# Log attention on one Trainium2 core: the weighted values of a step stand ahead of its second row of scores on TensorE

## The chip, the cores and the metric

One core of a Trainium2 chip runs the whole program in one launch. The metric is the device time of that launch in microseconds. Three runs of the kernel before were timed; one further execution was taken with the hardware profiler.

## What is computed

The reference is four layers on x of shape (8, 512, 128), float32, each on a layernorm and added to x: linear attention, an expert layer, log attention, and the same expert layer again. The change lies in log attention:

```python
L = jnp.einsum('bhqd,bhkd->bhqk', q, k) * scale
mask = jnp.tril(jnp.ones((t, t), dtype=L.dtype))[None, None]
L_y = jnp.einsum('bhqd,bhkd->bhqk', q, k_y) * scale
agg = jnp.sum(jnp.exp(jnp.clip(L_y, -15.0, 15.0)) * mask, axis=-1, keepdims=True) + EPS
r = jnp.log(jnp.abs(L) + EPS) - jnp.log(agg + EPS)
w = jax.nn.softplus(r) * mask
A = w / (jnp.sum(w, axis=-1, keepdims=True) + EPS)
out = jnp.einsum('bhqk,bhkd->bhqd', A, v)
```

with 16 heads of 8, and t = 512.

## The kernel before

Each engine has its own instruction list, written out by hand and tied together by semaphores. Log attention runs in steps: ten steps (`DUS`, i = 0 to 9) make a batch, and eight batches make 80 steps (`STEPS_A`). A step handles one or two blocks of keys by queries (`PIECES`) for all sixteen heads. There are two sides. Side A (step n) makes q.k_y scores: ScalarE takes their exp (`exponential`, L1717), VectorE clips it (`clip_exps`, L1835), POOL masks it (L1949), and two steps later TensorE sums it over the keys (`sum_exps`, L1620). Side B runs sixteen steps later (m = n - DUS - LAG) on q divided by those sums: VectorE takes the absolute value of the scores out of psum (`abs_scores`, L1843), ScalarE takes log(1 + .) (`logarithm`, L1723), POOL masks, and TensorE multiplies with the values and with ones (`weight_values`, L1636), two steps later still. The rings `ring_a` and `ring_b` hold three steps each.

Scores of a step come in two rows (`scores`, L1588, u = 0 and 1), for two heads of four each. A row of one side fills a pair of psum banks. As soon as side B runs (n of 16 and over), side A has only the pair 0 and side B only the pair 1 (`score_banks`), so each row waits in `wait_scores` until ScalarE's exp and VectorE's abs have read the row before. The text calls the rows S0 and S1.

At the end of most steps stands something for a neighbouring batch, all of it in bank 7, and each user waits for the reader of the one before (`wait_shared_bank`): at i = 0 `project` of q2 (L1653), at i = 1 `project_out` (L1676, behind VectorE's `scale_q`, L1857), at i = 2 `turn` (L1645, behind `add_output`, L1897), at i = 3, 4, 5 `project` of q, ky and k (L1653), at i = 6 `project_v` (L1658), at i = 8 `sum_prefix` (L1667). ScalarE and VectorE split the q, ky and k into two parts (`split_high` L1733, `split_low` L1850), at i = 4, 5, 6; VectorE's `split_low` stands behind its second abs of the step. At i = 8 VectorE's `empty` stands ahead of its first abs, at i = 9 `divide` and `correct` close the step, at i = 0 `add_routed` (L1360). The split parts go through DRAM: SP stores them (L1983) and loads them into `stacks` (L1988) in a fixed order, each behind a wait.

From n = 80 on (k = n - 80) side A is over. Each step then carries a piece of the second expert layer: ScalarE normalises (L872) and copies turned rows (L878, L881), VectorE takes their low part (L1114), TensorE turns rows in `lead_turn` (L697) and makes router logits in `lead_tensor` (L708), VectorE works out the routing from k = 8 to 10 (`rows_of`, L1275), and from k = 11 POOL sends the rows to their experts (L1002), each send with a short memset behind it (L467), 24 sends for a first chunk of rows and 24 for a second. On POOL `send` stands behind the masks of its step.

Of the kernel before, what the change touches and what calls it, by code (L numbers as in the profile page):

```python
# [86 lines left out]
def build(nc, x_in, ins, out):  # L87

    ctx = ExitStack()
    with ctx:  # L90
# [422 lines left out]
        class NothingFollows:  # L513
            takes_rest = False

            def tensor_step(self, pe, n):
                pass
# [938 lines left out]
        STEPS_A = B * DUS  # L1456
# [50 lines left out]
        class LogAttention:  # L1507
# [172 lines left out]
            def tensor_step(self, pe, n):  # L1680
                (a, i), m = divmod(n, DUS), n - DUS - LAG
                in_a, in_b = 0 <= n < STEPS_A, 0 <= m < STEPS_A
                self.scores(pe, n, m, 0)
                if 0 <= n - 2 < STEPS_A:
                    self.sum_exps(pe, n - 2)
                self.scores(pe, n, m, 1)
                if 0 <= n - STEPS_A:
                    self.following.lead_turn(pe, n - STEPS_A)
                if 0 <= m - 2 < STEPS_A:
                    self.weight_values(pe, m - 2)  # L1690
                if i == 0 and 0 <= a - 1 < B:
                    self.project(pe, "q2", a - 1)
                if i == 1 and 0 <= a - 3 < B:
                    self.project_out(pe, a - 3)
                if i == 2 and a + 1 < B:
                    self.turn(pe, a + 1)
                if i in (3, 4, 5) and a + 1 < B:
                    self.project(pe, ("q", "ky", "k")[i - 3], a + 1)
                if i == 6 and 0 <= a < B:
                    self.project_v(pe, a)  # L1700
                if i == 8 and 0 <= a - 1 < B:
                    self.sum_prefix(pe, a - 1)
                if 0 <= n - STEPS_A:
                    self.following.lead_tensor(pe, n - STEPS_A)
# [455 lines left out]
```

## Time and profile before

| | us |
|---|---|
| median of 3 runs | 1372.37 |
| lowest, highest | 1367.05, 1372.8 |
| profiled execution, its own time | 1369.74 |
| its span, first to last instruction | 1368.0 |
| TensorE matmul busy | 938.6 (69%) |
| VectorE busy | 675.0 (49%) |
| ScalarE busy | 595.1 (44%) |
| POOL busy | 538.3 (39%) |
| granted TensorE clock, mean | 0.82 |

Engines: PE is TensorE, PEld its weight loads, DVE VectorE, ACT ScalarE, POOL GpSimd, SPq the SyncE queue that issues DMAs. A row of a timeline has the start, the length, the engine, the line of the kernel, the operation and its operands, how many instructions were merged (x), and in brackets the idle time before it with what ended that time. Merged rows that follow one another overlap by some hundredths of a microsecond, so a stretch is taken from start to start. The granted clock is a share of full speed: 1.00 is 2.4 GHz, 0.50 is 1.2 GHz, and a figure between is a mean over a stretch with both.

### The profile page before, as it was taken

What the parts mean: (1) busy time and instruction counts of PE and PEld (TensorE: products, weight loads), DVE (VectorE), ACT (ScalarE), POOL (GpSimd) and SP (SyncE); (2) the same over time, 40 slices, a digit from 0 to 9 for tenths busy, and PEclk for the clock granted to TensorE, in tenths of its full rate; (3) what the DMA queues carried; (4) which work ended last, traced back from release to release, by engine and by line L of the source; (5) the groups of instructions that cost most, each with busy time, mean ns of one, the idle gap of its engine ahead of it and who ended that gap; (6) DMA issues with size and microseconds to landing.
All of it is one profiled execution on the core that took longest, in us unless ns stands there. A gap on an engine that the chain in (4) does not pass through costs nothing.

```text
span 1368.0 us, 19627 instructions
## 1 busy us (share of the span) xinstructions
PE 938.6 (69%) x6851; PEld 558.7 (41%) x6851; DVE 675.0 (49%) x1408; ACT 595.1 (44%) x853; POOL 538.3 (39%) x711
## 2 busy tenths in 40 slices
PE   4678538775947457787878787787676727359970
PEld 3556427553725123233333333333343515336650
DVE  4778413510213144787777877777558413202332
ACT  1222113232514356677776867786533214125430
POOL 1110670182181143464533333333216770421865
PEclk9877558896978576799999999999657868679985
DMA  9300020022321444353534343330200210032332
GB/s 288 93 1 1 29 63 1 23 64 77 93 57 58 141 149 154 129 163 126 172 121 147 106 155 121 138 113 27 70 8 24 66 35 9 17 89 85 101 83 77
DMA packets 101837, 118.88 MB, mean 87 GB/s; under 512 B 9328, under 2 KB 64112, under 8 KB 101616
## 3 DMA queue, kind: packets, MB, share of 16 engines
q1 hardware_dynamic: 74800, 91.54, 20.3%
q0 software_dynamic: 8192, 16.79, 4.1%
q10 hardware_dynamic: 18752, 9.31, 2.3%
q8 instruction: 59, 0.97, 0.3%
q14 instruction: 34, 0.28, 0.1%
HBM read 59.60 MB, written 58.00 MB: 86 GB/s over the span
## 4 chain that ended last, share of the span: by engine, by line
PE 34%; POOL 18%; DVE 15%; DMA 12%; issue 10%; SPq 6%; ACT 3%; another core or an unknown queue 0%; POOLq 0%; DVEq 0%; ACTq 0%
POOL x_sorted L1002 8%; DVE ring_b L1843 6%; PE psum L777 6%; POOL pause_room L467 5%; DMA stacks<-stack_qr 5%; PE psum L1636 4%; PE psum L1588 4%; POOL r_rows L1010 4%; SPq L1988 3%; SPq L1983 3%; PE psum L800 3%; PE psum L740 2%; PE psum L751 2%; DMA stack_q<-parts 2%; DMA stacks<-stack_ky 2%
## 5 line engine op out<-in xcount | busy, mean ns | idle before, releaser
L1843 DVE TENSOR_SCALAR ring_b<-psum 128x1024 int32<-128x1024 int32 x160 | 195.7, 1223 | 116.7 <-PE psum L1588 116.7
L1717 ACT ACTIVATE ring_a<-psum 128x1024 f32<-128x1024 f32 x160 | 163.2, 1024 | 151.0 <-PE psum L1588 149.2
L1588 PE MATMUL psum<-stacks 32*128 32x128 f32 (+3 forms) x1024 | 107.6, 401 | 138.1 <-DVE ring_b L1843 92.2
L1002 POOL DMA_INDIRECT x_sorted<-r_rows,rows_of x128 | 124.2, 970 | 171.2 <-DVE rows_of L1275 136.1
L1723 ACT ACTIVATE ring_b<-ring_b 128x1024 f32<-128x1024 f32 x160 | 168.5, 1054 | 48.1 <-DVE ring_b L1843 48.1
L1949 POOL TENSOR_SCALAR_AFFINE_SELECT ring_b<-ring_b 128x512 f32<-128x512 f32 (+1 forms) x112 | 82.1, 746 | 271.8 <-ACT ring_b L1723 271.4
L1010 POOL DMA_INDIRECT r_rows<-y_sorted,rows_of x128 | 128.7, 1005 | 141.6 <-DMA y_sorted<-y_out 110.5
L1588 PEld LDWEIGHTS psum<-stacks 32*128 32x128 f32 x1024 | 63.0, 202 | 235.9 <-issue 88.1
L1341 DVE TENSOR_TENSOR ring_b<-psum,ring_b 128x512 f32<-128x512 f32 x72 | 49.1, 683 | 211.7 <-ACT ring_b L904 192.4
L777 PE MATMUL psum<-w_expert,ring_a 128*128 x284 | 140.9, 619 | 5.2 <-issue 3.5
L1835 DVE TENSOR_SCALAR ring_a<-ring_a 128x1024 f32<-128x1024 f32 x160 | 121.2, 761 | 41.5 <-ACT ring_a L1717 41.3
L1949 POOL TENSOR_SCALAR_AFFINE_SELECT ring_a<-ring_a 128x512 f32<-128x512 f32 (+1 forms) x112 | 84.1, 764 | 75.6 <-DVE ring_a L1835 75.6
L1636 PE MATMUL psum<-ring_b,values 128*32 128x256 f32 (+3 forms) x1024 | 111.9, 514 | 0.0
L1636 PE MATMUL psum<-ring_b,ones_s 128*32 128x256 f32 (+3 forms) x1024 | 109.4, 504 | 0.0
L1620 PE MATMUL psum<-ring_a,ones_s 128*32 128x256 f32 (+3 forms) x1024 | 96.4, 487 | 3.2 <-POOL ring_a L1949 2.5
L740 PE MATMUL psum<-stacks,w_shared 128*128 128x512 f32 x168 | 51.9, 458 | 54.3 <-DVE ring_b L1332 30.9
L904 ACT ACTIVATE ring_b<-psum 128x512 f32<-128x512 f32 x72 | 42.5, 591 | 106.6 <-PE psum L777 104.5
L800 PE MATMUL psum<-w_expert,ring_b 128*128 x568 | 79.7, 285 | 6.3 <-issue 2.9
L467 POOL MEMSET pause_room<- 128x384 f32 x184 | 79.6, 432 | 0.2
L800 PEld LDWEIGHTS psum<-w_expert,ring_b 128*128 128x128 f32 x568 | 73.2, 201 | 7.3 <-issue 7.3
L777 PEld LDWEIGHTS psum<-w_expert,ring_a 128*128 128x128 f32 x284 | 50.6, 199 | 44.1 <-issue 44.0
L790 PEld LDWEIGHTS psum<-identity,ring_b 128*128 128x128 f32 x284 | 37.1, 148 | 65.7 <-issue 36.1
(205 smaller groups left out, 1350.5 us busy)
## 6 DMA issues: line engine op xcount, KB each, us to landing
ring_a<-x_sorted SPq DMA_DIRECT2D x34, 256.0 KB
y_sorted<-y_out ACTq DMA_DIRECT2D x34, 256.0 KB
stack_q<-parts SPq DMA_DIRECT2D x32, 256.0 KB
stack_ky<-parts SPq DMA_DIRECT2D x32, 256.0 KB
stacks<-stack_q SPq DMA_DIRECT2D x32, 256.0 KB
stacks<-stack_ky SPq DMA_DIRECT2D x32, 256.0 KB
stack_k<-parts SPq DMA_DIRECT2D x32, 256.0 KB
stacks<-stack_k SPq DMA_DIRECT2D x32, 256.0 KB
```

What stands on the lines that cost most here:

```text
L467: nc.gpsimd.memset(pause_room[:], 0.0).then_inc(paused, 1)
L777: mm = nc.tensor.matmul(bank(2 * (k % 2) + m), x_turned[:, n % 2, (i % 4) * 128:(i % 4 + 1) * 128], w["w_expert"][:, bass.ds(columns[m], 2 ...
L800: mm = nc.tensor.matmul(tiles(bank(4))[:, i % 4, :], hidden_turned[:, j % 2, at:at + 128], w["w_expert"][:, bass.ds(self.columns[j][m] + ( ...
L1002: nc.gpsimd.indirect_dma_start(out=x_sorted, out_offset=bass.IndirectOffsetOnAxis(ap=rows_of[:, n, at + t:at + t + 1], axis=0), in_=x_rows ...
L1010: nc.gpsimd.indirect_dma_start(out=fetched[:, b % 4, n, t, :], out_offset=None, in_=y_sorted[0:pages_of(self.last_of(self.chunk_ending(b)) ...
L1588: mm = nc.tensor.matmul(bank(2 * pair + j % 2)[:, column:column + width], keys[rows, s, kb * 128:(kb + 1) * 128], queries[rows, s, q0:q0 + ...
L1636: mm = nc.tensor.matmul(psum[32 * j:32 * j + 32, into, q0:q0 + width], weight, ring[:, m % RING, j, column:column + width], start=i == 0, ...
L1717: nc.scalar.activation(exps[:, n % RING, 2 * u:2 * u + 2, :], psum[:, first:first + 2, :], ACT.Exp, scale=SCALE).then_inc(self.exp, 1)
L1723: nc.scalar.activation(part, part, ACT.Ln, bias=1.0).then_inc(self.ln, 1)
L1835: nc.vector.tensor_scalar(part, part, CLIP_LO, CLIP_HI, ALU.max, ALU.min).then_inc(self.clip, 1)
L1843: nc.vector.tensor_scalar(ring[:, m % RING, HEADS_B[u][0]:HEADS_B[u][1] + 1, :].bitcast(I32), psum[:, first:first + 2, :].bitcast(I32), 0x ...
L1949: ins = nc.gpsimd.affine_select(out=part, in_=part, pattern=[[0, part.ap[1][1]], [1, 128]], compare_op=ALU.is_ge, fill=0.0, base=0, channe ...
```

## The change

`tensor_step` issues `weight_values` of step m - 2 right behind `sum_exps`, ahead of the second row of scores, where it stood behind that row and behind `lead_turn`. Nothing else is changed; the lists of the other engines are the same.

```diff
                 self.scores(pe, n, m, 0)
                 if 0 <= n - 2 < STEPS_A:
                     self.sum_exps(pe, n - 2)
+                if 0 <= m - 2 < STEPS_A:
+                    self.weight_values(pe, m - 2)
                 self.scores(pe, n, m, 1)
                 if 0 <= n - STEPS_A:
                     self.following.lead_turn(pe, n - STEPS_A)
-                if 0 <= m - 2 < STEPS_A:
-                    self.weight_values(pe, m - 2)
                 if i == 0 and 0 <= a - 1 < B:
                     self.project(pe, "q2", a - 1)
```

On TensorE, step n = 44 (i = 4) from the end of its first row of scores to the projection of ky; L1588 are scores, L1620 the sums, L1636 the weighted values. Before:

```order
L1588 MATMUL psum<-stacks 128x128 x2
L1620 MATMUL psum<-ring_a,ones_s 32x512 x4
L1588 MATMUL psum<-stacks 128x256 x2
L1588 MATMUL psum<-stacks 128x384 x2
L1588 MATMUL psum<-stacks 128x256 x2
L1588 MATMUL psum<-stacks 128x128 x2
L1636 MATMUL psum<-ring_b,values 32x384 x4
L1636 MATMUL psum<-ring_b,ones_s 32x384 x4
L1636 MATMUL psum<-ring_b,values 32x128 x4
L1636 MATMUL psum<-ring_b,ones_s 32x128 x4
L1653 MATMUL psum<-o_tok,b_ky 128x512
```

The same stretch of the change:

```order
L1588 MATMUL psum<-stacks 128x128 x2
L1620 MATMUL psum<-ring_a,ones_s 32x512 x4
L1636 MATMUL psum<-ring_b,values 32x384 x4
L1636 MATMUL psum<-ring_b,ones_s 32x384 x4
L1636 MATMUL psum<-ring_b,values 32x128 x4
L1636 MATMUL psum<-ring_b,ones_s 32x128 x4
L1588 MATMUL psum<-stacks 128x256 x2
L1588 MATMUL psum<-stacks 128x384 x2
L1588 MATMUL psum<-stacks 128x256 x2
L1588 MATMUL psum<-stacks 128x128 x2
L1653 MATMUL psum<-o_tok,b_ky 128x512
```

The sixteen matmuls of the weighted values went from behind the second row to ahead of it; only the projection is left between that row and the next step.

On TensorE, in the tail, step k = 5; L697 turns rows of the next layer, L708 makes its router logits. Before (the first row is both rows of scores):

```order
L1588 MATMUL psum<-stacks 128x512 x4
L697 MATMUL psum<-identity,r_rows 128x128 x4
L1636 MATMUL psum<-ring_b,values 32x512 x4
L1636 MATMUL psum<-ring_b,ones_s 32x512 x4
L708 MATMUL psum<-w_router,xT 128x8 x4
```

The same step of the change:

```order
L1588 MATMUL psum<-stacks 128x512 x2
L1636 MATMUL psum<-ring_b,values 32x512 x4
L1636 MATMUL psum<-ring_b,ones_s 32x512 x4
L1588 MATMUL psum<-stacks 128x512 x2
L697 MATMUL psum<-identity,r_rows 128x128 x4
L708 MATMUL psum<-w_router,xT 128x8 x4
```

The weighted values are no longer between the turned rows and the router logits.

## Rows read from the trace of the kernel before

**Rows 1.** The chain that ended last: share of the span by engine.

```profile
PE 34%; POOL 18%; DVE 15%; DMA 12%; issue 10%; SPq 6%; ACT 3%; another core or an unknown queue 0%; POOLq 0%; DVEq 0%; ACTq 0%
```

**Rows 2.** Waits of TensorE, 562 to 938 us: total, times, longest.

```profile
PE psum L1588 <- DVE ring_b L1843: 52.7, 55, 3.1
PE psum L1588 <- DMA stacks<-stack_qr: 11.3, 5, 3.7
```

**Rows 3.** Timeline of TensorE, step n = 44.

```profile
718.43 0.51 PE L1588 MATMUL psum<-stacks 32*128 32x256 f32 x8
718.87 1.06 PE L1620 MATMUL psum<-ring_a,ones_s 128*32 128x512 f32 x8
720.50 0.51 PE L1588 MATMUL psum<-stacks 32*128 32x256 f32 x8 [0.56 <-DVE ring_b L1843]
720.94 0.85 PE L1636 MATMUL psum<-ring_b,values 128*32 128x384 f32 x8
...
722.95 1.13 PE L1653 MATMUL psum<-o_tok,b_ky 128*128 128x512 f32 x2
724.01 0.51 PE L1588 MATMUL psum<-stacks 32*128 32x256 f32 x4
```

**Rows 4.** Timeline of VectorE, the same step.

```profile
721.08 1.23 DVE L1843 TENSOR_SCALAR ring_b<-psum 128x1024 int32<-128x1024 int32 x1 [0.23 <-PE psum L1588]
722.22 0.68 DVE L1850 TENSOR_TENSOR parts<-psum,parts 128x512 fp32r<-128x512 f32 x1
```

**Rows 5.** Timeline of TensorE, n = 51 (i = 1).

```profile
766.62 0.51 PE L1588 MATMUL psum<-stacks 32*128 32x384 f32 x8 [0.56 <-DVE ring_b L1843]
...
770.00 1.16 PE L1676 MATMUL psum<-b_proj,oT 128*128 128x128 f32 x8 [1.01 <-DVE w_a L1857]
```

**Rows 6.** Timeline of TensorE, n = 52 (i = 2).

```profile
773.17 0.51 PE L1588 MATMUL psum<-stacks 32*128 32x512 f32 x6 [0.58 <-DVE ring_b L1843]
...
776.72 0.66 PE L1645 MATMUL psum<-identity,x_hat 128*128 128x128 f32 x4 [1.18 <-DVE x_res L1897]
```

**Rows 7.** Timeline of TensorE, n = 38 (i = 8).

```profile
679.68 0.51 PE L1588 MATMUL psum<-stacks 32*128 32x384 f32 x6 [3.14 <-DVE ring_b L1843]
```

**Rows 8.** Windows behind gaps: length, busy times of five engines, PEclk, DMA share, GB/s.

```profile
615.50:620.50 5.00, 5.00 (x25) 1.65 (x26) 2.93 (x8) 3.21 (x4) 1.64 (x2) 0.66 0.59 206
...
808.30:813.30 5.00, 4.97 (x23) 1.63 (x24) 2.81 (x8) 3.21 (x4) 0.63 (x1) 0.50 0.26 96
...
884.10:889.10 5.00, 3.42 (x24) 1.05 (x24) 2.45 (x3) 1.97 (x2) 0.73 (x2) 1.00 0.26 101
```

**Rows 9.** Timeline of TensorE, tail: S1 of k = 2, step k = 5, k = 6, k = 9.

```profile
953.87 0.50 PE L1588 MATMUL psum<-stacks 32*128 32x384 f32 x4 [3.17 <-DVE ring_b L1843]
...
979.33 0.80 PE L1588 MATMUL psum<-stacks 32*128 32x512 f32 x2 [2.65 <-DVE ring_b L1843]
...
981.11 1.94 PE L1636 MATMUL psum<-ring_b,values 128*32 128x512 f32 x8
...
984.68 1.33 PE L708 MATMUL psum<-w_router,xT 128*128 128x8 f32 x8
985.94 0.50 PE L1588 MATMUL psum<-stacks 32*128 32x512 f32 x2
989.08 0.80 PE L1588 MATMUL psum<-stacks 32*128 32x512 f32 x2 [2.65 <-DVE ring_b L1843]
...
1020.53 0.50 PE L1588 MATMUL psum<-stacks 32*128 32x384 f32 x4 [1.33 <-DVE ring_b L1843]
```

**Rows 10.** Timeline of ScalarE, the same tail step.

```profile
981.50 1.65 ACT L872 ACTIVATE r_rows<-x_res,f_nbias,f_rstd 128x128 f32<-128x128 f32 x4 [1.13 <-DVE f_nbias L1107]
986.10 0.58 ACT L878 COPY xT<-psum 128x512 f32<-128x512 f32 x1 [2.95 <-PE psum L708]
```

**Rows 11.** Timeline of POOL: the first send and what follows the last.

```profile
1033.48 1.06 POOL L1002 DMA_INDIRECT x_sorted<-r_rows,rows_of  x1 [0.32 <-DVE rows_of L1275]
...
1124.28 1.04 POOL L991 TENSOR_TENSOR f_rstd<-f_var_eps,neg_half 128x4 f32<-128x4 f32 x1
```

## Prediction

> Steps are numbered n; i is n modulo 10, k is n - 80. S0 and S1 are the first and second row of scores on TensorE.
>
> **What bounds the kernel now.** I read the chain of waits first: no engine holds it for more than a third [rows 1]. Log attention (464 to 1070 us) is therefore read by itself. From 562 to 938 us TensorE's waits are mostly the score matmuls waiting for VectorE's abs over psum, 52.7 us, then 11.3 us for the loads of stack_qr [rows 2]. One step (n = 44) in the timeline shows the rhythm [rows 3]: S0 at 718.43, the exp sums at 718.87, a wait, S1 at 720.50, the weighted values at 720.94, the projection at 722.95, the next S0 at 724.01. So S0 to S1 takes 2.07 us though only 1.5 us of work lies there; that is the least a bank pair needs until VectorE's abs has emptied it. S1 to the next S0 takes 3.51 us and is full of work. Each row of scores needs such a cover, since from n = 16 on both rows of a step use the same two bank pairs.
>
> **The steady steps, n = 18 to 79.** The weighted values, 1.9 us [rows 3], leave the second cover for the first. No instruction is added and no DMA moves.
>
> S0 to S1 becomes 0.44 + 1.0 + 1.9 = 3.3 us in place of 2.07: +1.25 us in each step that is at this least. What comes back is S1 to S0:
> - i = 4, 5, 6: the projection into bank 7 waits until VectorE has taken the low part of the one before. That stands behind its second abs: abs at 721.08, low part at 722.22, over at 722.9 [rows 4], just when the weighted values ended. Half covered by chance, so nothing comes back: 3.5 us stays. +1.25 each.
> - i = 1: project_out waits for VectorE's scale_q; it started 3.38 us after S1 behind a wait of 1.01 [rows 5]. The wait grows, nothing comes back. +1.25. i = 2: the turn waits for add_output in the same way, 3.55 us after S1 [rows 6]. +1.25.
> - i = 3: 3.4 falls to the least of 2.07. -1.3 + 1.25, about 0.
> - i = 8: S1 waits 3.14 us, since VectorE does statistics and two additions ahead of its abs [rows 7]. The moved work fills a wait whose end VectorE sets: 0. After it the prefix sum still covers, so 1.85 comes back and 1.25 is paid at i = 9: -0.6.
> - i = 9 to 0 and 0 to 1: VectorE's divide, corrections and routed additions set the end: 0.
>
> A full batch: 5 x 1.25 - 0.6 = +5.6. Batches a = 3 to 6: 22.5. a = 2 has no project_out and a cheaper i = 2: 4.6. a = 7 has no projections at i = 3, 4, 5 (a third of these steps has nothing at its end and costs 1.0 each, for 2.3 falls only to 2.07): 3.5. a = 1: -0.5. **Sum +30.**
>
> SP's queue: its order is the same, and its loads hang on the low parts at i = 4. TensorE reaches i = 1 later relative to these, so part of the 11.3 us of waits for stack_qr goes; in a batch some 1.9 us falls in front of that S0, in three or four batches with a wait to take it: **-5**. The bounds are 0 and -11.3; I take the middle by that count.
>
> **TensorE's clock.** After waits of 2.2 us and over the granted clock often is the lower of its two levels. From 562 to 938 us nine gaps of 2.23 to 3.14 us were entered at 2.4 GHz; after six the next 5 us were granted 0.50 or 0.66 on average, after three 1.00 ([rows 8] shows the first, one at 0.50, and the last, which held). Three gaps of 1.63 left it at 1.00. The weighted values take 1.9 us at one level and 3.6 at the other [rows 3, 9], so a fall costs at least 1.7 us, more where other work follows; I take 2 for a new one. The six falls of today stand at i = 8 and i = 0 and cost six times 1.7. Their gaps close to 1.6 or under: **-10**. New gaps open in front of project_out (0.44 to 3.38 after S1: 2.9 us), the turn (3.1) and the projections at i = 4, 5, 6 (2.0 each). The first two are like those of 3.1, of which three of four fell: 2 x 0.8 x 2. Those of 2.0 lie between 1.63 (never) and 2.23 (three of five): 3 x 0.45 x 2. Together 5.9 a batch in a = 3 to 6, less in the others, some 28, of which the waits for stack_qr take a little: **+25**. Ends: 0 (none falls) and 50 (all do, with some 2.5 us each). Each follows on TensorE's own path, for S0 to S1 is now pure TensorE work.
> The Trainium skill (TensorE: Matmul & The Clock Gate, Why this matters for your kernels) warns only of idle gaps over about 3 us. By that rule nearly all the new gaps would leave the clock alone and this term would be near 0, which is rival 1; three of the five gaps of 2.23 us speak against it.
>
> **The tail, k = 3 to 15.** Here only the B side is left, and the next feed-forward layer's lead stands in the steps. From S1 of k = 2 (953.87) to S1 of k = 9 (1020.53) there are seven steps, 66.7 us [rows 9]. Step k = 5 to 6, 9.75 us, has this chain: S1 at 979.33, turn, weighted values 981.11 to 984.68, router logits, then ScalarE's copy of the turned rows at 986.10, which waited 2.95 us for those logits [rows 10], its second copy, VectorE's low part, abs, S1 at 989.08. The weighted values (3.6 us) lie ahead of the logits, and the chain behind the logits (3.1 us) hides nothing. Moved ahead of S1 they run beside that chain. ScalarE is busy with the normalised rows until 983.15, 3.8 us after S1 [rows 10]; 3.8 + 3.0 = 6.8 is one bound, TensorE's own work at the lower clock (3.0 + 0.7 + 3.6 = 7.3) the other. Five steps (k = 3 to 7) at 7.1, k = 8 (VectorE adds two additions) 8.1, k = 9 (first choice of experts on VectorE, prefix on TensorE) 8.5: 52.1. Gain 14.6. k = 10 is VectorE's (routing) and stays. Then POOL is the bound: it waited for rows_of at 1033.48 and then sent 48 tiles one after another until 1124.28 [rows 11], with TensorE idle behind it, so an earlier start is an earlier end: **-15**. Ends: 0 if something else holds POOL, -17.
>
> **Sum.** +30 - 5 - 10 + 25 - 15 = +25, against the profiled execution's own 1369.74 us (span 1368.0): **1395 us**. The median of the three runs shown is 1372.37, 2.6 above that execution; I leave the difference in the range.
>
> **Rivals.**
> 1. *The clock holds.* Gaps of 2.0 to 3.1 us don't lower it: 30 - 5 - 10 - 15 = 0, 1370 us. For it: three of nine did not. Against: six did, and a batch has five new ones. 0.12.
> 2. *The loads hide it (faster).* In the steady part a batch is then paced by the loads that end at the S0 of i = 1. Place: the wait for stack_qr; price: all 11.3 us of it swallow growth, and the clock holds; it decides where a batch grows by less than its wait (3.7 at most). 30 - 11.3 - 10 - 15, and 2 more in a tail at 2.4 GHz: -8, 1362 us. Against: several batches have no such wait. 0.06.
> 3. *The tail gives nothing.* POOL or VectorE starts the sends no earlier: 1410 us. 0.20.
> 4. *The clock stays low for whole batches.* Then S0 to S1 is 0.7 + 1.9 + 3.6 = 6.2, 2.8 more in some 28 steps, less the 25 counted: 1450 us. Against: in 562 to 938 the level always came back within some 7 us. 0.05.
>
> That the change does nothing is out: the order of TensorE's instructions differs in every step.
>
> **Numbers.** My case has 0.57. The range takes in rivals 1 and 3 and the bounds of the clock: 1366 to 1425. A difference of 0.5% (6.9 us) is about what can be told from none. Faster 0.07, same 0.13, slower 0.80.
>
> **What would show it.** S0 to S1 of 3.3 us in the steady steps and 3.5 behind it at i = 4 to 6; a new wait of projections for parts L1850, of project_out for 2.8 us; a mean clock under 1.00 behind them; n = 80 some 40 us later counted from n = 18 (389 us now) than before. In the tail steps of 7 us, and rows_of to the last send unchanged at 91 us. Wrong if the steady part grows by under 20 us, or if the tail keeps its steps of 9 to 10 us.

## The result and the profile after

| | before | after |
|---|---|---|
| median, us | 1372.59 (4 runs) | 1408.16 (4 runs, 1400.92 to 1411.69) |
| ratio, 95% interval | | 1.0252, 1.0197 to 1.0306 |
| profiled execution, own time | 1369.74 | 1407.53 |
| span | 1368.0 | 1405.8 |
| granted TensorE clock, mean | 0.82 | 0.814 |

The change is slower by 36 us; the forecast was slower by 25, 1395 in a range to 1425. The two traces are laid side by side by the starts of the score rows (L1588). Four stretches add up to the span:

| us | before | after | difference |
|---|---|---|---|
| start to S0 of n = 18 | 548.7 | 545.8 | -3.0 |
| steady: to S0 of n = 80 | 389.2 | 426.7 | +37.5 |
| tail: to S1 of n = 95 | 126.0 | 122.0 | -4.0 |
| from there to the end | 304.1 | 311.4 | +7.3 |

The prediction had the second at +40 and the tail at -15. The first stretch is untouched code; in the experiments below it lies between +1.6 and -9.0. The tail has a spread too: where its order was left as before (D, H and K below) it took 3.4 to 4.9 us more than in the one profiled execution before, so two profiles alone do not resolve a difference of that size.

The chain of waits after, by engine; beside [rows 1] TensorE has grown from 34 to 41%:

```profile
PE 41%; POOL 17%; DVE 12%; issue 12%; DMA 9%; SPq 5%; ACT 3%; another core or an unknown queue 0%; POOLq 0%; DVEq 0%; ACTq 0%
```

TensorE's waits after, 559 to 972 us (total, times, longest), to be read beside [rows 2]:

```profile
PE psum L1588 <- DVE ring_b L1843: 34.7, 32, 2.1
PE psum L1653 <- DVE parts L1850: 19.4, 10, 2.0
PE psum L1676 <- DVE w_a L1857: 12.9, 5, 2.6
PE psum L1588 <- DMA stacks<-stack_qr: 11.9, 4, 6.4
PE psum L1645 <- DVE x_res L1897: 10.3, 4, 2.6
PE psum L1658 <- DVE parts L1850: 9.6, 5, 1.9
PE psum L1636 <- DVE oT L1888: 7.0, 6, 1.7
```

The wait for VectorE's abs shrank, and waits of the projections, of project_out and of the turn stand in its place, as forecast. The wait for stack_qr is as it was. The last row was not forecast: weighted values now wait for `empty`.

One step, n = 44, in TensorE's timeline after (before: [rows 3]):

```profile
731.33 0.51 PE L1588 MATMUL psum<-stacks 32*128 32x256 f32 x8 [0.47 <-DVE ring_b L1843]
731.77 1.06 PE L1620 MATMUL psum<-ring_a,ones_s 128*32 128x512 f32 x8
732.65 0.83 PE L1636 MATMUL psum<-ring_b,values 128*32 128x384 f32 x8
...
734.49 0.51 PE L1588 MATMUL psum<-stacks 32*128 32x256 f32 x8
736.95 1.13 PE L1653 MATMUL psum<-o_tok,b_ky 128*128 128x512 f32 x2 [1.95 <-DVE parts L1850]
738.00 0.51 PE L1588 MATMUL psum<-stacks 32*128 32x256 f32 x6
```

S0 to S1 is 3.16 us (2.07 before), S1 to the next S0 3.51, as before, now with 1.95 us of it idle. This is the whole mechanism of the lost cover.

Steps n = 51 to 53 after show what the clock adds:

```profile
776.94 0.51 PE L1588 MATMUL psum<-stacks 32*128 32x384 f32 x8 [0.58 <-DVE ring_b L1843]
...
784.01 2.08 PE L1676 MATMUL psum<-b_proj,oT 128*128 128x128 f32 x8 [2.60 <-DVE w_a L1857]
786.01 0.80 PE L1588 MATMUL psum<-stacks 32*128 32x512 f32 x6
...
794.33 1.12 PE L1645 MATMUL psum<-identity,x_hat 128*128 128x128 f32 x4 [2.58 <-DVE x_res L1897]
795.38 0.80 PE L1588 MATMUL psum<-stacks 32*128 32x384 f32 x6
```

project_out took 1.16 us in [rows 5] and takes 2.08 here, the rows of scores 0.80 in place of 0.51: after gaps of 2.60 and 2.58 us TensorE runs at the lower level. S0 to S1 is then 5.24 and 5.67 us. In the change all five gaps of 2.55 to 2.60 in front of project_out were followed by a slow stretch, two of the four in front of the turn, and two of fifteen of 1.91 to 1.96 in front of the projections.

The step with i = 8, n = 58, after:

```profile
828.29 0.50 PE L1588 MATMUL psum<-stacks 32*128 32x384 f32 x6 [1.57 <-DVE ring_b L1843]
...
831.47 1.94 PE L1636 MATMUL psum<-ring_b,values 128*32 128x512 f32 x8 [1.68 <-DVE oT L1888]
...
834.94 0.51 PE L1588 MATMUL psum<-stacks 32*128 32x384 f32 x6
...
837.73 0.51 PE L1588 MATMUL psum<-stacks 32*128 32x512 f32 x6
```

Here a new batch of side B begins, and its first weighted values may not overwrite the bank until VectorE's `empty` (L1888) has read it. They now stand in front of S1: S0 to S1 is 6.65 us where it was 4.63. Most of the difference is again the clock: behind the gap of 1.68 us the sixteen weighted values take 3.47 us, at a granted clock of 0.52. In version J (below; its L1638 and L1590 are L1636 and L1588 here) the same gap at n = 48 left the clock at 1.00, and they take 1.86:

```profile
746.00 1.07 PE L1638 MATMUL psum<-ring_b,values 128*32 128x512 f32 x8 [1.68 <-DVE oT L1898]
...
747.86 0.50 PE L1590 MATMUL psum<-stacks 32*128 32x384 f32 x6
```

S0 to S1 is 5.05 there (4.64 before). So the wait for `empty` costs 0.4 us, and the lower clock another 1.6, at n = 38, 48 and 58 of the change.

In the tail, step k = 4 to 5, three engines after (TensorE, VectorE, ScalarE; before: [rows 9, 10]):

```profile
1004.28 1.11 PE L697 MATMUL psum<-identity,r_rows 128*128 128x128 f32 x4
1008.31 1.34 PE L708 MATMUL psum<-w_router,xT 128*128 128x8 f32 x8 [2.91 <-DVE ring_a L1136]
1009.58 0.79 PE L1588 MATMUL psum<-stacks 32*128 32x512 f32 x2
```

```profile
1007.47 0.38 DVE L1101 BATCH_NORM_AGGREGATE f_mean_var<-f_stats 128x2 f32<-128x6 f32 x4 [1.00 <-ACT r_rows L872]
...
1007.97 0.19 DVE L1136 TENSOR_TENSOR ring_a<-psum,router_bias 128x32 f32<-128x32 f32 x1
```

```profile
1005.73 1.65 ACT L872 ACTIVATE r_rows<-x_res,f_nbias,f_rstd 128x128 f32<-128x128 f32 x4 [2.03 <-DVE f_nbias L1107]
```

The logits wait 2.91 us for VectorE's copy of the logits of the batch before (L1136, 0.19 us of work), which stands behind the statistics, and these behind ScalarE's L872. S1 of k = 4 to S1 of k = 5 takes 10.3 us (9.4 before), and the next step, with the same wait, 10.4 (9.8 before).

POOL's first send and the row behind the last ([rows 11]); their distance is 93.1 us, 90.8 before:

```profile
1062.89 1.06 POOL L1002 DMA_INDIRECT x_sorted<-r_rows,rows_of  x1 [0.32 <-DVE rows_of L1275]
...
1156.01 1.04 POOL L991 TENSOR_TENSOR f_rstd<-f_var_eps,neg_half 128x4 f32<-128x4 f32 x1
```

### The profile page after: what moved, and what is told of

It is laid out like the page before. It is cut to its first block, busy times and chain, and to the rows that moved or that the text cites. A ratio compares the mean times of both kernels' runs of the same rounds, so it can differ in the third digit from the quotient of the medians.

```text
span 1405.8 us, 19627 instructions
## 1 busy us (share of the span) xinstructions
PE 942.1 (67%) x6851; PEld 568.0 (40%) x6851; DVE 662.4 (47%) x1408; ACT 598.4 (43%) x853; POOL 532.0 (38%) x711
## 4 chain that ended last, share of the span: by engine, by line
PE 41%; POOL 17%; DVE 12%; issue 12%; DMA 9%; SPq 5%; ACT 3%; another core or an unknown queue 0%; POOLq 0%; DVEq 0%; ACTq 0%
PE psum L1636 8%; POOL x_sorted L1002 8%; PE psum L777 6%; PE psum L1588 5%; POOL pause_room L467 5%; PE psum L1620 4%; POOL r_rows L1010 4%; DMA stacks<-stack_qr 3%; PE psum L800 3%; DVE ring_b L1843 3%; SPq L1988 2%; SPq L1983 2%; PE psum L740 2%; PE psum L751 2%; DMA stacks<-stack_ky 2%
## 5 line engine op out<-in xcount | busy, mean ns | idle before, releaser
L1843 DVE TENSOR_SCALAR ring_b<-psum 128x1024 int32<-128x1024 int32 x160 | 195.5, 1222 | 172.2 <-PE psum L1588 166.6
L1010 POOL DMA_INDIRECT r_rows<-y_sorted,rows_of x128 | 126.4, 988 | 145.1 <-DMA y_sorted<-y_out 110.3
L1588 PE MATMUL psum<-stacks 32*128 32x128 f32 (+3 forms) x1024 | 110.0, 408 | 104.4 <-DVE ring_b L1843 58.4
L1588 PEld LDWEIGHTS psum<-stacks 32*128 32x128 f32 x1024 | 63.6, 205 | 203.1 <-issue 86.3
L1835 DVE TENSOR_SCALAR ring_a<-ring_a 128x1024 f32<-128x1024 f32 x160 | 112.3, 705 | 41.4 <-ACT ring_a L1717 41.2
L1636 PE MATMUL psum<-ring_b,values 128*32 128x256 f32 (+3 forms) x1024 | 111.4, 512 | 12.9 <-DVE oT L1888 9.5
L1636 PE MATMUL psum<-ring_b,ones_s 128*32 128x256 f32 (+3 forms) x1024 | 109.4, 503 | 0.0
L1949 POOL TENSOR_SCALAR_AFFINE_SELECT ring_a<-ring_a 128x512 f32<-128x512 f32 (+1 forms) x112 | 78.3, 713 | 76.5 <-DVE ring_a L1835 76.5
L1620 PE MATMUL psum<-ring_a,ones_s 128*32 128x256 f32 (+3 forms) x1024 | 104.6, 522 | 2.1 <-POOL ring_a L1949 1.4
L790 PEld LDWEIGHTS psum<-identity,ring_b 128*128 128x128 f32 x284 | 37.8, 150 | 67.0 <-issue 37.2
```

The lines of the kernel that those rows point to most:

```text
L1010: nc.gpsimd.indirect_dma_start(out=fetched[:, b % 4, n, t, :], out_offset=None, in_=y_sorted[0:pages_of(self.last_of(self.chunk_ending(b)) ...
L1588: mm = nc.tensor.matmul(bank(2 * pair + j % 2)[:, column:column + width], keys[rows, s, kb * 128:(kb + 1) * 128], queries[rows, s, q0:q0 + ...
L1620: mm = nc.tensor.matmul(psum[32 * j:32 * j + 32, 4, q0:q0 + width], ones_s[:, s, :], exps[:, n % RING, j, column:column + width], start=i ...
L1636: mm = nc.tensor.matmul(psum[32 * j:32 * j + 32, into, q0:q0 + width], weight, ring[:, m % RING, j, column:column + width], start=i == 0, ...
L1843: nc.vector.tensor_scalar(ring[:, m % RING, HEADS_B[u][0]:HEADS_B[u][1] + 1, :].bitcast(I32), psum[:, first:first + 2, :].bitcast(I32), 0x ...
L1949: ins = nc.gpsimd.affine_select(out=part, in_=part, pattern=[[0, part.ap[1][1]], [1, 128]], compare_op=ALU.is_ge, fill=0.0, base=0, channe ...
```

## The experiments

In each, `ahead` says in which steps the weighted values stand in front of S1; elsewhere they stand as before. The added lines shift the line numbers: in C and J TensorE's L1590, L1638, L1647 and L1678 are L1588, L1636, L1645 and L1676, in the others VectorE's L1846 and L1853 are L1843 and L1850. The edit that all share:

```diff
+                ahead = ...
+                if 0 <= m - 2 < STEPS_A and ahead:
+                    self.weight_values(pe, m - 2)
                 self.scores(pe, n, m, 1)
                 if 0 <= n - STEPS_A:
                     self.following.lead_turn(pe, n - STEPS_A)
-                if 0 <= m - 2 < STEPS_A:
+                if 0 <= m - 2 < STEPS_A and not ahead:
                     self.weight_values(pe, m - 2)
```

All in one table. The ratio is to the kernel before on the same chip; steady and tail are the differences to before of the stretches above, in each one's profiled execution.

| | steps ahead, and what else | ratio (95%) | steady | tail |
|---|---|---|---|---|
| change | all | 1.025 (1.020-1.031) | +37.5 | -4.0 |
| A | tail only | 0.993 (0.989-0.996) | -1.3 | -6.6 |
| B | all but i = 8 | 1.033 (1.028-1.037) | +43.3 | -5.7 |
| C | all, gaps filled | 1.009 (1.006-1.013) | +13.9 | -4.3 |
| D | i = 4, 5, 6 | 1.012 (1.007-1.017) | +16.0 | +4.1 |
| E | all, logits first | 1.019 (1.013-1.025) | +36.5 | -11.4 |
| F | tail, logits first | 0.992 (0.989-0.995) | -1.7 | -10.7 |
| G | tail, i = 0, 8, logits first | 0.989 (0.983-0.995) | -6.8 | -13.4 |
| H | i = 8 | 0.997 (0.994-1.000) | -8.9 | +4.9 |
| I | G with later loads | 1.012 (1.008-1.016) | +23.2 | -12.9 |
| G again | as G | 0.988 (0.984-0.993) | -9.7 | -12.9 |
| J | all, filled, logits first | 1.001 (0.998-1.003) | +13.9 | -10.7 |
| K | i = 3, 7, 9 | 1.007 (1.004-1.010) | +9.7 | +3.4 |

**C, the clock term.** `ahead = True`, a tile `nil` that POOL sets to zero at the start, and at the end of the step:

```diff
+        FILLS = {1: (3, 3, 7), 2: (3, 3, 6), 4: (2, 2, 6), 5: (2, 2, 6), 6: (2, 2, 6)}
+                if in_b and i in FILLS and FILLS[i][1] <= a <= FILLS[i][2]:
+                    for _ in range(FILLS[i][0]):
+                        for j in range(4):
+                            nc.tensor.matmul(psum[32 * j:32 * j + 32, 5, 0:T], nil[:], const["reaches"][:], start=False,
+                                             stop=False, skip_group_check=True, tile_position=(0, 32 * j))
```

> As the change, with matmuls of a tile of zeros into bank 5 added where TensorE idles at i = 1 (three sets of four), i = 2 (three) and i = 4, 5, 6 (two) of the steady batches; a set of four of 128x512 takes 0.85 to 0.9 us at 2.4 GHz. They fill the new gaps of 2.0 to 3.1 us and add nothing to the sums. Clock theory (the prediction's term of +25): the first halves of over 4 us behind i = 1 and i = 2 go back to 3.2, some 15 falls of 1 to 2.5 us each, 20 to 25 us less than the change: about 1385. Rival (the clock's falls in the gaps cost nothing, the growth is the lost cover alone): no faster than the change, 1408 or later by what the added matmuls delay, some 5 us.

The same steps, n = 51 to 53, with the gaps filled:

```profile
767.35 2.78 PE L1699 MATMUL psum<-reaches,nil 128*32 128x512 f32 x24
770.07 1.16 PE L1678 MATMUL psum<-b_proj,oT 128*128 128x128 f32 x8
771.15 0.51 PE L1590 MATMUL psum<-stacks 32*128 32x512 f32 x6
...
774.76 2.78 PE L1699 MATMUL psum<-reaches,nil 128*32 128x512 f32 x24
777.47 0.66 PE L1647 MATMUL psum<-identity,x_hat 128*128 128x128 f32 x4
778.06 0.51 PE L1590 MATMUL psum<-stacks 32*128 32x384 f32 x6
```

More work on TensorE, and less time: project_out is back at 1.16 us, the turn at 0.66, S0 to S1 of both following steps at 3.17. The steady part grows by 13.9 us in place of 37.5: 23.6 us of the change's growth were the clock's, as the clock theory expected (20 to 25). The falls behind the gap of 1.68 us at i = 8 are still in C (S0 to S1 of 6.6 to 6.8 at n = 38, 48 and 58). The window of 560 to 980 us, first of the change, then of C (length, busy times of five engines, PEclk, DMA share, GB/s):

```profile
560.00:980.00 420.00, 313.98 (x3336) 145.76 (x3334) 281.00 (x414) 286.26 (x340) 147.55 (x198) 0.91 0.34 117
```

```profile
560.00:980.00 420.00, 360.03 (x3926) 159.20 (x3922) 296.15 (x456) 300.77 (x365) 155.28 (x205) 0.95 0.35 121
```

The rival, that these falls cost nothing, is out.

**D, the lost cover alone.** `ahead = n < STEPS_A and i in (4, 5, 6)`

> The change alone at the steady steps with i = 4, 5, 6; all else as before, the tail too. Cover theory: S0 to S1 goes from 2.07 to 3.16 in each, nothing comes back behind, so +1.1 each in some 14 to 16 steps: +16 to +18, 1389. With clock falls in the gaps of 2.0 us (the prediction's 0.45 x 2 each) another +13: 1402. Rival (later steps or the wait for stack_qr at i = 1 swallow it): +6 or less.

S0 to S1 grew by 1.08 to 1.14 us in fifteen of the eighteen steps. Up to n = 66 nothing came back; at n = 74 to 76, which have no projection behind S1, 3.1 us did. S1 of n = 54 to the next S0 in D:

```profile
791.46 0.51 PE L1588 MATMUL psum<-stacks 32*128 32x256 f32 x8
793.92 1.13 PE L1653 MATMUL psum<-xT,b_ky 128*128 128x512 f32 x2 [1.95 <-DVE parts L1853]
794.97 0.51 PE L1588 MATMUL psum<-stacks 32*128 32x256 f32 x4
```

The clock fell behind one of the fifteen gaps of 1.91 to 1.96 (batches 2 to 6), and also behind gaps of 1.56 and 1.52 in front of S0 of n = 75 and 76, where S0 to S1 is 4.84 and 4.85. The steps i = 4, 5 and 6 cost 21.9 us together: 17 of lost cover, the cover theory's number, and 5 of clock where it said 13. That the steady part comes to +16.0 as well is luck: i = 0 gave 9.7 back, because TensorE waited less for stack_qr (3.9 us over the steady part, 11.3 before) and the clock held behind the gaps of 2.24 at n = 50 and 60, and i = 3 and 8, left as before, cost 5.1 more.

**B and H, the new wait at i = 8.** `ahead = n >= STEPS_A or i != 8`, and `ahead = n < STEPS_A and i == 8`

> As the change, but at the steady steps with i = 8 the order is that of before. Theory A: in the change the weighted values of i = 8 wait for VectorE's empty (L1888) of the same step and stand in front of S1, which made S0 to S1 there 6.65 us where it was 4.65 (+2 us in five or six batches); with the old order that part goes, 9 to 10 us, and the second half at i = 8 comes back to 4.6 or above, which returns up to 1.8 per batch. So between 1398 and 1408, I take 1403, with S0 to S1 at i = 8 back at 4.65. The prediction's price for i = 8 (0 at S1, gain behind it): taking it out changes i = 8 and 9 by 0.6 a batch to the worse, 1411.

> The change alone at the steady steps with i = 8, all else as before. Theory 1 (missed wait): weighted values wait for empty in front of S1, +2.0, and give 1.85 back behind it: 0. Theory 2 (clock): in addition the gap of 2.23 us behind S1, with a fall in most batches (S1 to S0 6.2 to 7.6 instead of 4.64), is gone: -1.6 to -3 in four or five batches, -8 to -12, ratio 0.992 to 0.994; the second of these is what putting i = 8 back in the change pointed at (4.2 us later than the change at n = 95).

B missed: S0 to S1 at i = 8 came back to 4.4, yet the kernel lost another 5.9 us in the steady part, on the side that the prediction's own price had pointed to. The same step n = 58 in B:

```profile
832.15 0.80 PE L1588 MATMUL psum<-stacks 32*128 32x384 f32 x6 [2.92 <-DVE ring_b L1846]
832.88 1.94 PE L1636 MATMUL psum<-ring_b,values 128*32 128x512 f32 x8
...
836.45 3.29 PE L1667 MATMUL psum<-reaches,v_tok 128*128 128x512 f32 x8
839.67 0.51 PE L1588 MATMUL psum<-stacks 32*128 32x512 f32 x6
```

Without the moved work the gap in front of S1 is one piece of 2.92 us, the clock falls, and S1 to S0 is 7.52 us (2.79 in the change). With the move the weighted values fill part of that wait; what is left is a gap of 1.68, behind which only they ran slowly. At i = 8 B takes 16.5 us more than the change, of which i = 0 gives 7.5 back. H shows the move alone: S0 to S1 +0.6 in most batches (+2.2 at n = 48, where the clock fell behind the gap of 1.88), S1 to S0 -1.9 where the clock held before and -3.4 to -4.8 where it fell, 13.9 us over the batches. Part of it goes again, 3.7 between S0 of i = 0 and S0 of i = 1 and 1.3 in the other steps, so the steady part has 8.9; the tail, in the old order, was 4.9 longer in H's profiled execution. The ratio (0.994 to 1.000) is therefore just short of telling H from no change.

**K, the steps priced at nothing.** `ahead = n < STEPS_A and i in (3, 7, 9)`

> The change alone at the steady steps with i = 3, 7 and 9, the tail as before. Prediction: i = 3 gives back what it costs (first half +1.1, second half -1.3), i = 7 is swallowed by the wait that VectorE ends at i = 8, i = 9 by the one at i = 0: 0 in all, ratio 0.998 to 1.002. Rival from the change's own steps (first halves of i = 7 and 9 +1.1 each with only 0.2 back, nothing absorbed behind): +1.7 a batch, +10, 1.007.

The rival's total holds, with other parts. i = 3 is even (+0.6 in all). i = 7 costs 5.1 over the batches and i = 9 costs 5.7, as the rival said. But i = 0 gave 5.9 back and i = 1 another 2.1, and i = 8 costs 6.7 more: S1 to S0 is over 6 us there in all seven batches, where it was in four before, since the clock fell more often. Whether i = 0 absorbed what i = 9 cost, as the prediction had it, is not shown: i = 0 moved by +0.1 to -9.7 in A, D and F too, which change nothing at i = 9 and 0. K around i = 7 to 8, n = 57 and 58:

```profile
796.98 0.51 PE L1588 MATMUL psum<-stacks 32*128 32x512 f32 x6
...
800.14 0.51 PE L1588 MATMUL psum<-stacks 32*128 32x512 f32 x6
802.21 0.51 PE L1588 MATMUL psum<-stacks 32*128 32x384 f32 x6 [1.56 <-DVE ring_b L1846]
```

S0 to S1 3.16 (2.09 before), S1 to S0 2.07 (2.30 before), a net +0.85, and the following S0 to S1 falls only from 4.63 to 4.43.

**A, E and F, the tail.** `ahead = n >= STEPS_A` in A; in E and F also this on VectorE:

```diff
+                if 1 <= k - 3 <= self.early:
+                    self.vector_logits_of(v, k - 3)
                 if 1 <= k <= self.early:
                     self.vector_bias(v, k)
                 if 1 <= k + 1 <= self.early:
                     self.vector_stats(v, k + 1)
-                if 1 <= k - 3 <= self.early:
-                    self.vector_logits_of(v, k - 3)
```

> The weighted values stand ahead of S1 only from n = 80 on; n < 80 is the order of before. Theory A (read from the trace of after: the tail's steps are now held by VectorE's logit_ready, L1136, which stands behind bias and statistics): the tail shortens by about 5 us as it did in after (shift of S1 against before +37.4 at n = 80, +32.1 at n = 89), so about 1367 against 1372, ratio 0.996. Prediction's own term: -15, 1357. Rival B: once n < 80 is as before, the tail is held elsewhere and gives 0.

> As the change, with VectorE's copy of the router logits (L1136) moved to the front of its lead work in a step. Theory A: in the tail of the change TensorE's logits wait for that copy of the batch before (14.2 us over 8 waits on the row L708 <-DVE ring_a L1136), which stands behind bias and statistics; S1 to S0 at k = 4 and 5 is 6.0 to 6.1 us there and 3.3 at k = 6. With the copy first, k = 4 and 5 fall towards 3.3 to 4.5: 4 to 6 us less than the change, ratio to before 1.021 (1.025 for the change). Rival B: ScalarE's copy of the normalised rows (L872) sets the end of these steps as well, and the copy moved forward gives 0 to 1 us.

> The tail alone in the new order (n from 80 on), n < 80 as before, and the copy of the logits first on VectorE. The tail alone gave 8.0 us at S1 of n = 89 and 0.993. Theory A adds 4 to 6: 0.989 to 0.990, 1353. Rival B adds nothing: 0.993.

A is the half of the change that helps: 0.993, and its interval (0.989 to 0.996) lies below 1. TensorE's waits of this kind in 967 to 1046 us of the change, and in 965 to 1040 of E:

```profile
PE psum L708 <- DVE ring_a L1136: 7.3, 4, 2.9
```

```profile
PE psum L708 <- DVE ring_a L1136: 3.4, 4, 0.9
```

and k = 4 to 5 in E:

```profile
1000.56 0.66 PE L697 MATMUL psum<-identity,r_rows 128*128 128x128 f32 x4
1002.15 1.56 PE L708 MATMUL psum<-w_router,xT 128*128 128x8 f32 x8 [0.93 <-DVE ring_a L1136]
1003.64 0.79 PE L1588 MATMUL psum<-stacks 32*128 32x512 f32 x2
```

S1 to S0 is 3.5 and 3.3 us at k = 4 and 5, where it was 6.0 and 6.1. From S1 of k = 2 to S1 of k = 9: 66.7 before, 61.2 in the change, 60.1 in A, 54.5 in E, 55.1 in F. The move of one operation of 0.19 us gives back 6.7 of the missing 9.1 us. In the medians F stands at 0.992 beside A's 0.993: the difference of the two is not resolved; E beside the change (1.019, 1.025) points the same way, with intervals that overlap.

**J, both costs out.**

> The change with both of its avoidable costs taken out: the matmuls of zeros in the new gaps of the steady batches, and the copy of the logits first on VectorE. What is left is the lost cover alone against the whole gain of the tail. If the terms add: the filled version gave 1.009, the copy first took 0.006 off the change, so 1.003, 1369 to 1372; at S1 of n = 80 +14 us against before, at n = 95 about 0. Rival (they overlap: the earlier tail meets a clock or a wait that the copy can't help): 1.009 again.

1.0005 (0.998 to 1.003). The terms add: what is left of the change is +13.9 us from n = 18 to 80 (the lost cover, less what i = 8 and i = 0 gave, with the falls of the clock that stayed) against -10.7 in the tail, and the two nearly cancel.

**G and I, what can be kept.** G is `ahead = n >= STEPS_A or i in (0, 8)` with the logits first; I adds to it

```diff
+                        if b > 0:
+                            sp.wait_ge(self.abs, 2 * (DUS * (b - 1) + 5) + 1)
                         self.load_a(sp, a, 1)
```

> New order in the tail and at the steady steps with i = 0 and i = 8 alone, logits first. Theory: at i = 0 VectorE sets the end of S0 to S1 (3.75, in the change 3.54), so the weighted values move there free, S1 to S0 falls from 5.0 or more to 2.15 and the gap of 2.23 with its clock falls closes; the step behind pays up to 1.9 as i = 1's first half did in the change. At i = 8 S0 to S1 grows by 2.0 (the wait for empty, L1888) and S1 to S0 falls from 4.64 (6.1 to 7.6 with a fall) to 2.8: net -2 to -3 where the clock fell, 0 where it held. Over the batches -10 to -18 on top of the tail: 0.977 to 0.983, about 1342. Rival: the growth at i = 8 and i = 1 takes it all back, 0.989.

> The same kernel as e9_tail_logits_0_8, timed in more rounds and beside e12_loads_later on one chip: 0.989 again if the first ratio (0.983 to 0.995) was right.

> As the version with i = 0 and i = 8 in the new order, the tail too and the logits first; in addition SyncE's loads of the second half of A's stacks (stack_q, stack_ky, groups 2 and 3), which stand in the queue right behind the four loads that S0 of i = 1 waits for, wait for VectorE's first abs of that step. In the version without this wait S0 at i = 1 waits 34.0 us in all for stack_qr (11.3 in the kernel before), and the four loads issued from 608 to 615 us end only at 628.9, together with the four behind them. Theory A (the eight transfers share the bandwidth): alone the four land some 5 us earlier, most of the 34 us goes, less what the later loads cost at i = 5: 10 to 20 us under the version without it, 1330 to 1340, ratio 0.972 to 0.98. Theory B (the transfers end in the order of their issue, so those behind cost nothing): no gain, 0.989, or slower where i = 5 now waits.

G beats both kernels, 0.988 (0.984 to 0.993) in the longer measurement, less than the 0.977 to 0.983 expected. TensorE's longest sum of waits there, 536 to 924 us, and the row of n = 31:

```profile
PE psum L1588 <- DMA stacks<-stack_qr: 34.0, 7, 8.2
```

```profile
628.90 0.80 PE L1588 MATMUL psum<-stacks 32*128 32x384 f32 x8 [6.95 <-DMA stacks<-stack_qr]
```

What i = 8 and i = 0 gain, TensorE waits for at i = 1: 34.0 us in place of 11.3 (27.6 in the second measurement of G). This is the pace of the loads that rival 2 spoke of, met from the other side. Version I missed: its theory A was wrong. The four loads did not land sooner. S0 of n = 31 could start 14.1 us after the last of them was issued in G (614.80) and 14.0 in I (627.06), and over the six batches it was 13.4 to 14.6 us in both. That the four ended together with the four behind them, as the expectation has it, no row shows. The same row in I, and S0 of i = 6, which now waits for a late load:

```profile
641.04 0.80 PE L1588 MATMUL psum<-stacks 32*128 32x384 f32 x8 [5.73 <-DMA stacks<-stack_qr]
...
673.31 0.80 PE L1588 MATMUL psum<-stacks 32*128 32x384 f32 x6 [2.62 <-DMA stacks<-stack_qr]
```

The transfers behind the four cost them nothing, and putting them later cost 30 us of the steady part (33 against the second measurement of G): the waits for stack_qr came to 55.2 us in twelve places. What would make the chain of stores and loads shorter stays open.

## Why the prediction held, and where it did not

The side was right, and so were both mechanisms, the lost cover and the clock. The size was 11 us short by the medians and 13 by the profiles (+37.8 for +25): the tail gave 11 less than said, the steady part cost 2.5 less, and stretches that the change does not touch added 4. By its steps:

- **S0 to S1 of 3.3, +1.25 a step.** Measured 3.16, +1.10; from start to start the exp sums take 0.88 (said 1.0) and the weighted values 1.84 (said 1.9). At i = 4, 5, 6 nothing came back, as said. The projection's new wait was 1.95 (said 2.0), that of project_out 2.6 (said 2.8).
- **Steady +30, -5, -10, in sum +15.** With the gaps at i = 1, 2, 4, 5 and 6 filled (C) it was +13.9. The sum is right, its parts are not, so the agreement is partly luck. Over all batches in C: i = 1 to 6 +27.3, near the terms for these steps; i = 9 +5.9, near its term; i = 7 +5.1, which the sum did not price at all; at i = 8 S0 to S1 +11.5 where it said "0". The prediction missed that the wait for `empty` on L1636 now stands in front of S1. That wait itself is 0.4 a step; the rest is weighted values at the lower clock, behind its gap of 1.68 and at n = 18 and 78. Against these S1 to S0 gave 20.9 at i = 8 and 15.5 at i = 0. There the step said that VectorE sets the end; but that holds for S1 alone, and the weighted values left the stretch behind it. "-5" for the waits for stack_qr did not come in the change (11.3 before, 11.9 after), but A and F, whose steady steps are those of before, had 6.4 and 7.5, and B, D and K 2.5 to 4.6, so one pair of profiles does not settle it.
- **Clock +25.** 23.6 by C against the change, by place differently from what was said. The steps in which gaps in front of project_out and the turn took effect (i = 1, 2, 3) hold 18.8 of it (said: 16), those of the projections 3.1 (said: some 12); chances of 0.45 for gaps of 2.0 were too high, two of fifteen fell. Of the -10 for the falls at i = 8 and i = 0 the premise held and the conclusion did not: their gaps closed to 1.57 and 1.68 us, but the clock still fell behind such gaps, at n = 38, 48 and 58, at n = 30 (S0 to S1 4.85, where 3.54 is usual) and at n = 78 (5.20, also 3.54 elsewhere). The prediction's count of gaps also left out those that end with a load: in the trace of before one of 1.89 us, in front of S0 of n = 71 at 889.44, was followed by 5 us at 0.66.
- **Tail -15.** This is the step that failed. S1 of k = 2 to S1 of k = 9 came to 61.2, not 52.1. The sum took ScalarE and TensorE as the two bounds of a step and left out that the logits of one batch wait for VectorE's copy of those before. With the copy first (E) it is 54.5, and 53.7 in G: the price was near for a kernel in which that wait is gone. From S0 of n = 80 to S1 of n = 95 the tail gave 4.0.
- **Behind the tail** rows_of to the last send was to stay at 91 us and is 93.1. Another 6.1 us came later, in code that the change does not touch; some 4 of it is one pause of POOL near the end, 4.19 us in front of a gather (L1010) at 1377.29, that the trace puts down to no other engine. Such pauses of 1.6 to 6.2 us stand there in B, I and the second measurement of G as well, and none before. From S1 of n = 95 to the end it was +7.3 in the change, +3 to +5 in B, E and G, +9.5 in I, and within about 1 us of before in the others. What decides it stays open.
- **Rivals.** Rival 1 (the clock holds) is what C and J were built to be: it is out for the change. The Trainium skill (TensorE: Matmul & The Clock Gate, Why this matters for your kernels) warns of idle gaps of over about 3 us; here 23.6 us were lost behind gaps of 2.6 us and less, so the measurement decides against that rule as a safe bound. Rival 3 (the tail gives nothing, 1410) was nearest to the time, nearer than the case taken (1395), though for another reason: the sends did begin earlier, by 5.1 us counted from S0 of n = 80, and the tail gave 4 of its 15. Rivals 2 and 4 did not come about.

## What to carry to other kernels

Work that stands between two rows which share a buffer is cover for the reader; before it moves, look at what will fill its old place. If that is only a wait, the move costs its length, and a TensorE gap of some 2.5 us there can cost more than the cover did, so matmuls that add zero made the changed kernel faster. When a chain is shortened, list for every instruction in it all semaphores that it waits for, those long satisfied too, for one of them is the next bound: here a copy of 0.19 us held back half of a gain. And undo a change step by step: its half in the tail was a gain, and a version that keeps that and two of the ten steps is 1.2% faster than the kernel before.

## What the hardware showed that was not expected

The length of a gap alone does not tell whether the granted clock falls. Gaps of 2.57 and 2.58 us in front of the turn were followed by a slow stretch in two of four batches of the change. In B three steps near n = 75, with gaps of 1.51 to 1.55 us in front, ran S0 to S1 at 4.85 us; in the change the same steps, with the same gaps, took 3.15 to 3.16. The prediction had read three gaps of 1.63 as a length that never falls. The gap of 1.68 at i = 8 was followed by a fall at n = 38 and 58 of J and not at n = 48. One slow stretch can also be short: at n = 58 of the change, behind two gaps of 1.57 and 1.68 us, only the weighted values ran slowly, 3.47 us in all.
